# Softmax sums of an attention kernel: GpSimd's partial sum joins one DMA accumulation chain, and one count a unit replaces three

## The reference, cut to what matters

```
def _attention(q, k, v, bias):
    scores = jnp.einsum('bhqd,bhkd->bhqk', q, k) / jnp.sqrt(jnp.float32(hd))
    if bias is not None:
        scores = scores + bias[None, None]
    attn = jax.nn.softmax(scores, axis=-1)
    return jnp.einsum('bhqk,bhkd->bhqd', attn, v)

out_short = _attention(q, k_s, v_s, decay_bias)
out_long = _attention(q, k_l, v_l, None)
out = alpha * out_short + (1.0 - alpha) * out_long
```

## Time and profile before

| | us |
|---|---|
| median of 3 runs | 5075.12 (5067.31 to 5075.18) |
| profiled execution, its own time | 5071.46 |
| its span, first to last instruction | 5069.4 |
| PE busy | 4808.1 |
| DVE busy | 4044.8 |
| POOL busy | 3012.3 |
| ACT busy | 2998.2 |

### The profile page before, as it was taken

One profiled execution on the slowest core, in us unless ns is written; L12 is line 12 of the kernel. 1 busy time (PEld: TensorE's weight loads), 2 busy tenths in 40 slices (PEclk: granted clock), 3 DMA queues, 4 the chain that ended last, 5 costly groups with the idle time before them and its releaser, 6 DMA issues. The chain is left out here.

```text
span 5069.4 us, 101554 instructions
## 1 busy us (share of the span) xinstructions
PE 4808.1 (95%) x31276; PEld 2103.4 (41%) x31276; DVE 4044.8 (80%) x6613; ACT 2998.2 (59%) x5234; POOL 3012.3 (59%) x1267
## 2 busy tenths in 40 slices
PE   6888799999999999999999999999999599999998
PEld 3443233333333333333333333333332377777776
DVE  5556688888888888888888888888886388888887
ACT  2222166777676777777777777776767355555554
POOL 0000067878788888888887878888888233333332
PEclk9999789999999999999999999999999699999999
DMA  4332356777677776767676767777666200000000
GB/s 144 117 117 87 108 128 168 170 176 170 173 166 177 169 173 167 174 170 172 168 170 173 171 172 167 175 171 172 166 164 152 85 24 26 26 26 26 20 28 11
DMA packets 216978, 661.83 MB, mean 131 GB/s; under 512 B 38099, under 2 KB 111955, under 8 KB 158997
## 3 DMA queue, kind: packets, MB, share of 16 engines
q0 software_dynamic: 64512, 469.79, 39.8%
q1 hardware_dynamic: 151957, 185.66, 12.2%
HBM read 123.56 MB, written 61.64 MB: 37 GB/s over the span
## 5 line engine op out<-in xcount | busy, mean ns | idle before, releaser
L852 DVE TENSOR_REDUCE rowmax_parts<-scores_qk 128x1 f32<-128x512 f32 x4096 | 2524.6, 679 | 463.7 <-PE scores_qk L925 463.7
L832 ACT ACTIVATE probs_T<-scores_kq 128x512 f32<-128x512 f32 x4096 | 2286.3, 596 | 979.3 <-PE scores_kq L925 915.8
L766 POOL TENSOR_TENSOR probs_added<-probs_added,probs_T 128x2048 f32<-128x2048 f32 x448 | 2030.1, 4531 | 459.2 <-ACT probs_T L832 447.8
L925 PE MATMUL scores_kq<-q_operand,k_operand 103*128 103x512 f16 (+3 forms) x3712 | 1274.7, 349 | 10.2 <-ACT probs_T L832 8.3
L925 PE MATMUL scores_qk<-k_operand,q_operand 96*128 96x512 f16 (+4 forms) x3712 | 1123.1, 352 | 43.2 <-DMA k_operand<-positions_dram 19.4
L996 PE MATMUL outputs_T<-probs_T,v_operand 128*32 128x512 f32 x8192 | 1091.9, 605 | 1.3 <-ACT probs_T L832 1.3
L925 PEld LDWEIGHTS scores_kq<-q_operand,k_operand 103*128 103x128 f16 x3712 | 358.7, 97 | 920.9 <-ACT probs_T L832 635.7
L925 PEld LDWEIGHTS scores_qk<-k_operand,q_operand 96*128 96x128 f16 (+1 forms) x3712 | 354.8, 98 | 438.3 <-DVE rowmax_parts L852 184.4
L1602 PE MATMUL f_gate_up<-w_gate_up,xq_T 128*128 128x256 f16 (+1 forms) x4608 | 494.1, 265 | 8.6 <-DVE hidden L1493 7.5
L1602 PEld LDWEIGHTS f_gate_up<-w_gate_up,xq_T 128*128 128x128 f16 x4608 | 421.2, 98 | 77.8 <-issue 25.4
L766 POOL TENSOR_TENSOR probs_added<-probs_T 128x2048 f32<-128x2048 f32 x64 | 290.2, 4535 | 238.4 <-ACT probs_T L832 238.4
(11 more groups left out here) (165 smaller groups left out, 4302.1 us busy)
## 6 DMA issues: line engine op xcount, KB each, us to landing
probs_poured<-probs_T POOLq DMA_DIRECT2D x448, 1024.0 KB, 7.2
qk_parts_dram<-qk_parts SPq DMA_DIRECT2D x96, 256.0 KB, 2.5
q_operand<-qk_parts_dram SPq DMA_DIRECT2D x192, 128.0 KB, 2.6
k_operand<-qk_parts_dram SPq DMA_DIRECT2D x192, 128.0 KB, 3.1
v_dram<-v_heads SPq DMA_DIRECT2D x16, 1024.0 KB, 5.7
v_operand<-v_dram SPq DMA_DIRECT2D x64, 256.0 KB, 6.3
q_operand_above<-qk_parts_dram SPq DMA_DIRECT2D x96, 128.0 KB, 2.8
x_groups<-x SPq DMA_DIRECT2D x8, 1024.0 KB, 9.6
```

Of the source, the lines that this page charges most:

```text
L766: nc.gpsimd.tensor_tensor(total, first, probs[:, b % PBUF, :], ALU.add).then_inc(added.sem, 1)
L832: nc.scalar.activation(probs[:, kb % PBUF, qt * BANK:(qt + 1) * BANK], pb[:, k % 2, :], ACT.Exp)\
L852: nc.vector.reduce_max(rowmax[:, w % 2, c // NQ, c % NQ:c % NQ + 1], pa[:, k % 3, :], AX.X)\
L925: return nc.tensor.matmul(out, lhsT, rhs, start=start, stop=stop, skip_group_check=True)
```

## The change

- The blocks are dealt anew: six go by DMA, in one chain (0, 3, 6, 9, 12, 15); ten are POOL's, in nine adds. `probs_poured` has two buffers, one for even and one for odd units, and two semaphores.
- `merge`: a seventh DMA of the chain adds POOL's sum to the chain's. POOL issues it in the next unit ahead of block MERGE = 4, after a wait for the chain's sixth link.
- `count`: PE counts once a unit, the merged sum, in step 7 of the next unit (COUNT = KB + 7), after a wait for the seventh link.
- `take_sums` is gone, with the SBUF tiles `sums_T` and `sums_inverse`: DVE's reciprocals read the PSUM bank and write in place, in steps 8 to 11, and `weigh` reads them from PSUM in step 12.
- `mix` is POOL's now, after every second unit, ahead of block 14.

```
-INVERT = 5
-WEIGH = 10
-MIX = 11
-
-
-BY_POOL = (0, 1, 3, 5, 7, 9, 11, 13, 14)
-BY_DMA = ((2, 6, 10), (4, 8, 12, 15))
+INVERT = 8
+WEIGH = 12
+MIX = 14
+
+
+BY_DMA = (0, 3, 6, 9, 12, 15)
+BY_POOL = tuple(b for b in range(KB) if b not in BY_DMA)
 ADDS = len(BY_POOL) - 1
-POURS = [len(blocks) for blocks in BY_DMA]
-COUNT_POURED = (14, KB + 3)
-COUNT_ADDED = KB + 1
-TAKE_SUMS = 5
+POURS = len(BY_DMA) + 1
+MERGE = 4
+COUNT = KB + 7
...
         def _(pool):
-            give_credit(pool, [maxed, expd, summed, added, counted, taken, sums_out, weighed] + counted_poured + stored)
+            give_credit(pool, [maxed, expd, summed, added, counted, taken, weighed] + stored)
...
-                if b == 1:
-                    first = probs[:, 0, :]
+                if b == BY_POOL[1]:
+                    first = probs[:, BY_POOL[0], :]
                     wait_apart(pool, counted, counted.at(n, w - 1), passed)
                 else:
                     first = total
                     wait_apart(pool, added, added.at(n, w * ADDS + adds_until(b) - 1), passed)
                 nc.gpsimd.tensor_tensor(total, first, probs[:, b % PBUF, :], ALU.add).then_inc(added.sem, 1)
 
-            def pour(w, n, b, c):
-
-                i = BY_DMA[c].index(b)
+            def pour(w, n, b):
+
+                i = BY_DMA.index(b)
+                total, landed = poured_sum[:, w % 2, :], poured[w % 2]
                 wait_apart(pool, expd, expd.at(n, (w * KB + b + 1) * NQ), passed)
                 if i == 0:
-                    wait_apart(pool, counted_poured[c], counted_poured[c].at(n, w), passed)
-                    nc.gpsimd.dma_start(poured_sum[c][:, :], probs[:, b % PBUF, :]).then_inc(poured[c].sem, 16)
+                    wait_apart(pool, counted, counted.at(n, w - 1), passed)
+                    nc.gpsimd.dma_start(total, probs[:, b % PBUF, :]).then_inc(landed.sem, 16)
                 else:
-                    wait_apart(pool, poured[c], poured[c].at(n, w * POURS[c] + i), passed)
-                    nc.gpsimd.dma_start(poured_sum[c][:, :], probs[:, b % PBUF, :], accum_op=ALU.add)\
-                        .then_inc(poured[c].sem, 16)
-
-            def one_pass(n):
+                    wait_apart(pool, landed, landed.at(n, w // 2 * POURS + i), passed)
+                    nc.gpsimd.dma_start(total, probs[:, b % PBUF, :], accum_op=ALU.add).then_inc(landed.sem, 16)
+
+            def merge(w, n):
+
+                landed = poured[w % 2]
+                wait_apart(pool, added, added.at(n, (w + 1) * ADDS), passed)
+                wait_apart(pool, landed, landed.at(n, w // 2 * POURS + len(BY_DMA)), passed)
+                nc.gpsimd.dma_start(poured_sum[:, w % 2, :], added_sum[:, w % 2, :], accum_op=ALU.add).then_inc(landed.sem, 16)
+
+            def mix(p, n):
+
+                wait_apart(pool, weighed, weighed.at(n, 2 * p + 2), passed)
+                wait_apart(pool, stored[p], stored[p].before(n, NQ), passed)
+                nc.gpsimd.tensor_tensor(o_mix[:, p, :], o_w[:, 0, :], o_w[:, 1, :], ALU.add).then_inc(mixed.sem, 1)
+
+            def one_pass(n, first, last):
                 for w in range(UNITS):
-                    for b in range(1, KB):
-                        if b in BY_POOL:
+                    back = unit_before(w, n, first)
+                    for b in range(KB):
+                        if b == MERGE and back:
+                            merge(*back)
+                        if b == MIX and back and back[0] % 2:
+                            mix(back[0] // 2, back[1])
+                        if b in BY_DMA:
+                            pour(w, n, b)
+                        elif b != BY_POOL[0]:
                             add(w, n, b)
-                        else:
-                            pour(w, n, b, int(b in BY_DMA[1]))
-
-            with nc.Fori(0, PASSES // 2, engines=[pool.engine], hint_back_edge=True) as m:
-                for i in range(2):
-                    one_pass(m * 2 + i)
+
+            one_pass(0, True, False)
+            with nc.Fori(0, (PASSES - 2) // TURN, engines=[pool.engine], hint_back_edge=True) as m:
+                for i in range(TURN):
+                    one_pass(m * TURN + (i + 1), False, False)
+            one_pass(PASSES - 1, False, True)
+            merge(UNITS - 1, PASSES - 1)
+            mix(1, PASSES - 1)
...
-                            c = int(b in BY_DMA[1])
-                            act.wait_ge(poured[c].sem, poured[c].at(n, u * POURS[c] + BY_DMA[c].index(b) + 1))
+                            landed = poured[u % 2]
+                            act.wait_ge(landed.sem, landed.at(n, u // 2 * POURS + BY_DMA.index(b) + 1))
...
             def invert(w, n, r):
 
-                dve.wait_ge(sums_out.sem, sums_out.at(n, w + 1))
-                nc.vector.reciprocal(inv[:, r * P:(r + 1) * P], sums[:, r * P:(r + 1) * P]).then_inc(inverted.sem, 1)
+                dve.wait_ge(counted.sem, counted.at(n, w + 1))
+                nc.vector.reciprocal(pc[:, r * P:(r + 1) * P], pc[:, r * P:(r + 1) * P]).then_inc(inverted.sem, 1)
 
             def weigh(w, n):
 
                 dve.wait_ge(taken.sem, taken.at(n, w + 1))
                 dve.wait_ge(inverted.sem, inverted.at(n, (w + 1) * NQ))
-                nc.vector.scalar_tensor_tensor(o_w[:, w % 2, :], oT[:, w % 2, :], gates[:, 3 + w % 2:4 + w % 2], inv[:, :],
+                if w == 2:
+                    dve.wait_ge(mixed.sem, mixed.at(n, 1))
+                elif w == 0 and (not isinstance(n, int) or n > 0):
+                    dve.wait_ge(mixed.sem, mixed.before(n, 2))
+                nc.vector.scalar_tensor_tensor(o_w[:, w % 2, :], oT[:, w % 2, :], gates[:, 3 + w % 2:4 + w % 2], pc[:, :],
                                                ALU.mult, ALU.mult).then_inc(weighed.sem, 1)
...
-                        if back and i == MIX and back[0] % 2:
-                            mix(back[0] // 2, back[1])
...
+            def count(w, n):
+
+                landed = poured[w % 2]
+                pe.wait_ge(weighed.sem, weighed.at(n, w))
+                pe.wait_ge(landed.sem, landed.at(n, (w // 2 + 1) * POURS))
                 for qt in range(NQ):
-                    mm = nc.tensor.matmul(pc[qt * HD:(qt + 1) * HD, :], ones[:, :], src[:, qt * BANK:(qt + 1) * BANK],
-                                          start=first, stop=last)
-                mm.then_inc(done.sem, 1)
-
-            def count_poured(w, n, c):
-
-                if c == 0:
-                    pe.wait_ge(sums_out.sem, sums_out.at(n, w))
-                pe.wait_ge(poured[c].sem, poured[c].at(n, (w + 1) * POURS[c]))
-                count(poured_sum[c], counted_poured[c], c == 0, c == 1)
-
-            def count_added(w, n):
-
-                pe.wait_ge(added.sem, added.at(n, (w + 1) * ADDS))
-                count(added_sum[:, w % 2, :], counted, False, False)
-
-            def counts(w, n, i):
-
-                for c in range(2):
-                    if i == COUNT_POURED[c]:
-                        count_poured(w, n, c)
-                if i == COUNT_ADDED:
-                    count_added(w, n)
+                    last = nc.tensor.matmul(pc[qt * HD:(qt + 1) * HD, :], ones[:, :],
+                                            poured_sum[:, w % 2, qt * BANK:(qt + 1) * BANK], start=True, stop=True)
+                last.then_inc(counted.sem, 1)
...
-                        counts(w, n, i)
-                        if back:
-                            counts(*back, KB + i)
+                        if back and KB + i == COUNT:
+                            count(*back)
...
+            count(UNITS - 1, PASSES - 1)
```

More of the change, by code:

```diff
@@ L619, in attend @@
         added_sum = sb("probs_added", [P, 2, L], F32)
-        poured_sum = [sb(f"probs_poured{i}", [P, L], F32) for i in range(2)]
+        poured_sum = sb("probs_poured", [P, 2, L], F32)
         rowmax = sb("rowmax_parts", [P, 2, KB, NQ], F32)
@@ L652, in attend @@
         added = Rises(sem("a_added"), UNITS * ADDS, credit=1)
-        poured = [Rises(sem(f"a_poured{i}"), UNITS * POURS[i], 16) for i in range(2)]
+        poured = [Rises(sem(f"a_poured{i}"), UNITS // 2 * POURS, 16) for i in range(2)]
         counted = Rises(sem("a_counted"), UNITS, credit=1)
-        counted_poured = [Rises(sem(f"a_counted_poured{i}"), UNITS, credit=1) for i in range(2)]
         taken = Rises(sem("a_o_taken"), UNITS, credit=1)
-        sums_out = Rises(sem("a_sums_out"), UNITS, credit=1)
         inverted = Rises(sem("a_inverted"), UNITS * NQ)
@@ L812, in one_pass @@
                 for w in range(UNITS):
-                    back = unit_before(w, n, first)
                     for kb in range(KB):
-                        if back and kb == TAKE_SUMS:
-                            take_sums(*back)
                         if kb == (TURN_MAX + 2) % KB and after(w, n, last):
@@ L879, in weigh @@
                 dve.wait_ge(inverted.sem, inverted.at(n, (w + 1) * NQ))
```

(42 more changed lines are left out.)

7 lines of the change are left out of this document (removed).

## The result

The new kernel takes 5362.0 us (median of 4 runs, 5355.2 to 5371.7) against 5071.2 (5066.5 to 5075.2) for the one before on the same chip: a ratio of 1.0575, 95% interval 1.0554 to 1.0596. It is 291 us slower. The forecast was 4991, with 5065 as its upper end.

A forecast was written before the change was run, and what follows sets the result against it. PE was taken to bound most steps and DVE four; -107.5 (counts) + 6 (PSUM) + 9.5 (waits) + 9.8 (tail) = -82 us gave 4991 us, from 5071.5 profiled and a median of 5075.1; range 4956 to 5065.

The forecast's parts named there:

- The new waits: PE's wait in step 7 for the merge's landing: between none and 0.7 us a unit, taken as 0.15, 9.5 us in all.
- the forecast unit: Mean length of a unit after the change: 1.72 us less from counts, 49.70, with units near 49.9 as a sign.
- Counts, -107.5: On PE, three counts a unit become one: 125 counts fewer at 0.86 us each, 107.5 us less.
- Reciprocals and `weigh` from PSUM, +6: DVE's cost of reading and writing PSUM: between 0 and 25 us, taken as 6.
- The estimate of 65 ns each: Fixed DVE cost of 120 cycles from PSUM against 58 from SBUF: 0.065 us each, 16 us in all; not adopted.
- DVE against POOL in `weigh`: Rival: `weigh` in step 12 blocks during POOL's add, some 3 us a unit, 5179 us; chance 4 in 100.
- POOL's sum: POOL's adds, DMAs and `mix` take 48.0 us of a 49.70 us unit, 97%, so POOL just keeps up.
- hidden cost: Extra time of a POOL add straight behind a DMA: 0 to 0.40 us for each of seven, taken as 0 to 0.2.
- POOL becomes the bound: Rival: each DMA costs POOL's next add 0.40 us, a unit takes 50.8, the kernel 5043 us; chance 2 in 10.
- `mix`: On POOL, 512 columns take 1.13 us, 1.31 with waiting, every second unit; leaving DVE gains 0.
- the merge lands late: Rival: a queue's accumulation begins only when the other has landed; PE waits 2.4 us a unit, 5125 us; 12 in 100.
- the likeliest case: Merge data follow pour 3's in the queue, landing 4.50 us later than alone, PE waiting 0.2 us; chance 58 in 100.

The follow-up runs named there:

- merge first: Tried first: the change with the merge issued ahead of block 3, not block 4, so ahead of pour 3 in the queue: 5246.9 us, ratio 1.035.
- count late: The change with PE's count in step 10, not 7, reciprocals and `weigh` three steps later, `mix` ahead of block 15: 5280.7 us, ratio 1.0417.
- last pour earlier: The change with block 14 in the DMA chain and block 15 in POOL's adds: 5328.0 us, ratio 1.0509.
- add 13 away: The change with block 13, an add ahead of pour 15, left out of the sums: 5267.5 us, ratio 1.0387.
- add 2 away: The change with block 1 left out of the sums, so without the add ahead of pour 3: 5358.3 us, ratio 1.0557.
- breaking the loop at pour 0: The change with block 0 left out of the sums, so the DMA chain begins with pour 3: 5003.5 us, ratio 0.9874.
- room everywhere: The change with block 14 in the chain, merge ahead of block 5, count in step 9; fastest seven-link arrangement with the whole sum: 5143.5 us, ratio 1.0147.
- the version with two chains: The kernel before, both chains kept, POOL's sum joined to the chain of three, two counts a unit, reciprocals and `weigh` from PSUM: 5021.1 us, ratio 0.9903.
- the kernel before with one count less: The kernel before without the count of POOL's sum, whose nine blocks are then missing from the sums: 5016.9 us, ratio 0.9895.

## Why the prediction was wrong, point by point

**The step that failed is "The new waits".** It put pour 3 at t = 10.13 and the merge at 11.0, its landing at 21.6, and PE's wait at 0.15 us a unit, the +9.5 us of the sum, where PE's count was measured to wait 301.8. Measured in the odd unit above: merge issued at 16.26, landed at 29.06, wait 7.45. The 7.45 us are two terms. 5.3 us of them (16.26 - 11.0) come from what I left out: pour 3 waits for pour 0's landing. In the old order the first pour of a chain was blocks 2 and 4, each with the adds and pours of several steps before its next link; in the new one it leaves 0.58 us behind the last pour of the other chain, lands after 13.0 us, or 9.6 in the even unit, and the next link is due 10 us after a unit's start. I had even computed that POOL would send pour 15 at 2.0 us into the next unit, and didn't ask what pour 0, behind it, would then do. The other 2.2 us are the landing: 12.8, for which 21.6 - 11.0 = 10.6 stood. Together 7.5, as PE asked at 21.6, near the forecast 21.4. In the even unit the merge left at 11.8 and landed 11.7 later; a wait of 1.53.

**The wait feeds itself.** I wrote the times of one unit with its start as given. But what stands behind PE's count (steps 8 to 15), and behind those POOL's adds, decides when pour 15 leaves, and so when pour 0 lands. That no shift of one wait was worth its full size (merge first 115 us, count late 81, last pour earlier 34, add 13 away 95, add 2 away nothing) and that breaking the loop at pour 0 was worth 359 bears this out. It gives the members of the loop, not their prices: the theory's own forecasts missed by 133 us (room everywhere, 5010), 77 (without pour 0, 5080) and 177 (without the add of block 13, 5090).

**The price.** By windows, a unit has 5.57 us of idle PE (49.6 / 500 x 56.16) against 0.40 before, and 50.6 us of busy PE (450.36 / 500 x 56.16) where the forecast unit had 51.02 - 1.72 = 49.3. The first is the wait of 4.66 and half a us around it; the second, 1.3 us, comes with the clock: it was granted in full in 3000 to 3500 before, 0.95 after, that is for part of the time at the lower of its two levels, and the count after the wait of 7.45 took 1.94 us, the one after 1.53 took 1.07. 5.2 + 1.3 = 6.5 against the 6.3 us by which the unit (56.16) missed the forecast (49.85). I had no term for the clock. Where the wait was gone (the change without its first pour, the version with two chains) the clock was back at 0.975 and 0.976 for the whole run.

**Counts, -107.5:** not seen by itself in the change, but the kernel before with one count less gained 50.6 us of the 54 that the same price gives. The change without its first pour kept the full set of savings and lay 66 us under before with 75.7 us of POOL's and 17.3 of PE's waits still in its stretch; that fits the size, roughly, and doesn't measure it.

**Reciprocals and `weigh` from PSUM, +6:** 956 ns for 942, and 739 for 742. 14 ns x 4 x 62 = 3.5 us, inside the bounds. The estimate of 65 ns each, worked out from the Trainium skill, "VectorE: DVE Perf Modes", in the section on the errata of SBUF sources, is not borne out.

**DVE against POOL in `weigh`:** with one tensor in PSUM it never lasted longer than 741 ns in 45 times, and in each of the 45 an add of POOL was under way. That rival is refuted, as by the rule of the Trainium skill, "SBUF — State Buffer", section "Who interferes with whom". With `mix` on DVE, both inputs in SBUF, it took 1162 ns in the median and 1771 at most, where it took 681 before, with the add of POOL over about 0.1 us after its start. The first two lines are of the change, an add of POOL and a `weigh` inside it; the last two are of the run with `mix` on DVE, where `mix` ends at 1366.59, 0.55 us behind the add:

```profile
2034.66 4.54 POOL L761 TENSOR_TENSOR probs_added<-probs_added,probs_T 128x2048 f32<-128x2048 f32 x1 [0.18 <-POOL probs_added L761]
2037.61 0.73 DVE L891 SCALAR_TENSOR_TENSOR o_weighed<-o_T,gates,sums 128x512 f32<-128x512 f32 x1
...
1361.27 4.77 POOL L761 TENSOR_TENSOR probs_added<-probs_added,probs_T 128x2048 f32<-128x2048 f32 x1
...
1365.42 1.17 DVE L889 TENSOR_TENSOR o_mixed<-o_weighed 128x512 f32<-128x512 f32 x1
```

**POOL's sum:** right. A round of two adds and a pour without a wait took 10.08 us (2097.22 to 2107.30; forecast 10.06). POOL was busy for 47.0 us a unit (2067.28 us from 1026.6 to 3497.5, 44 units); the forecast was 48.0. An add behind a pour is recorded 0.3 us longer (4.83 from 2039.74) but starts 0.60 after the pour did (2039.14), not 0.88; from that pour to the end of the add are 5.43 us, against 0.88 + 4.53 = 5.41, so there is no hidden cost. The rival "POOL becomes the bound" falls with it: with 288 us of its adds taken away, from the best arrangement, 37 came back.

**`mix`,** 1.47 us recorded, forecast 1.13; on DVE or POOL made no difference.

**The rival "the merge lands late"** ends on the right side, with a landing that PE waits for, and it said 2.4 us a unit and 5125. That the pour in front of it delays the merge is shown by the first experiment (12.0 against 8.4 in the median); it was a third of the matter. Of the two ways in which I had priced it, neither fits alone: pour 3 landed 7.0 us after its issue in both units, and the merge 6.6 us after that in the odd unit and 5.4 in the even one, between the 4.5 of the likeliest case and the 7.0 of this rival. I had priced one landing and no more.

**Left open.** In odd units the first pour is slow with the last one 0.58 us ahead of it (13.0 us) and nearly as slow with it 5.1 us ahead (12.0, in the run with the last pour earlier), with SP's loads beside it in both; in even units it takes 9.6 and 5.8 to 7.1. What SP's loads do alone wasn't tried, nor why the merge takes 12 to 13 us behind a pour that itself takes 7.0. And no version was tried that keeps the change's single count and gives its first pour room everywhere without a wait.

## What to carry to other kernels

A chain of DMAs in one queue has to be costed link by link, in the order of the queue: what lies unlanded ahead of each link, when it lands, and which in-order engine stands at the next link until then. Write that round the loop over units, from the last link of one to the first of the next, because a wait there delays its own cause. Two short chains with several steps between landing and use saved one count a unit at nearly no wait, and the gain was what a count is worth (0.9903). The single long one saved two counts and lost six times as much to its waits (1.0575).

## What the runs showed of the hardware that was not expected

A 1 MB DMA that adds into SBUF, issued 0.75 us behind another in POOL's queue, took 12.0 us to land in the median, and 7.3 to 9.8 in five units where the one in front had left 7.7 to 9.5 us earlier. A plain copy of 1 MB, issued 5.1 us behind a pour, took 12.0 us among ten loads of SP's, and 5.8 to 7.1 behind seven that had been issued before it. A reciprocal of 128 columns took 14 ns more in PSUM than in SBUF (956 for 942). An add of 512 columns on DVE with both inputs in SBUF, started during an add of POOL, took 1162 ns in the median for 681. A wait of PE of 7.45 us was followed by a count at half speed (1.94 us for 1.07), one of 1.53 us was not.
